# Splitting the weighted hidden block in the third and fourth layers' experts: VectorE writes the f16 first part of odd blocks itself

## The reference

```python
# L2: 14 experts, 128 -> 256 -> 128, one expert a token
logits = x @ router_w
assignments = argmax(logits); weights = softmax(logits)[assignments]
hid = gelu(einsum('nd,edf->nef', x, w1) + b1)
all_out = einsum('nef,efd->ned', hid, w2) + b2
moe_out = all_out[assignments] * weights
# L3: 8 experts, 128 -> 256 -> 128, two experts a token
h1 = gelu(einsum('bsd,edf->ebsf', mla_out, w1) + b1)
h2 = einsum('ebsf,efd->ebsd', h1, w2) + b2
moe_out = einsum('bse,ebsd->bsd', combine, h2)
# and for both: x = x + tanh(g_ffn[l]) * ...
```

## Time and profile before

| What | us |
|---|---|
| Median of 3 runs | 1422.92 |
| Lowest and highest of them | 1414.69, 1425.28 |
| The profiled execution, its own time | 1416.76 |
| Its span, first to last instruction | 1415.0 |
| First and last activation of the third layer's experts | 842.1, 1003.6 |
| First and last activation of the fourth layer's experts | 1313.7, 1402.6 |

### The profile page before, as it was taken

One profiled execution on the slowest core, in us unless ns is written; L12 is line 12 of the kernel. 1 busy time (PEld: TensorE's weight loads), 2 busy tenths in 40 slices (PEclk: granted clock), 3 DMA queues, 4 the chain that ended last, 5 costly groups with the idle time before them and its releaser, 6 DMA issues. The chain is left out here.

```text
span 1415.0 us, 30558 instructions
## 1 busy us (share of the span) xinstructions
PE 1113.4 (79%) x10422; PEld 531.6 (38%) x10422; DVE 909.6 (64%) x1691; ACT 786.6 (56%) x1467; POOL 551.7 (39%) x604
## 2 busy tenths in 40 slices
PE   2668767886299999998577759999868856777897
PEld 1334444444234444444222333333434532234333
DVE  3768648885656676666689534445668757983454
ACT  1257412773255555554178548888527723883886
POOL 1205102541145555554135127787401201211686
PEclk7779967998599999999689969999969985997999
DMA  8731004100044434442711023223142013100432
GB/s 250 252 131 34 2 1 151 41 26 1 7 134 132 127 123 132 125 129 67 245 32 32 2 40 90 92 93 91 64 163 63 3 47 108 45 17 2 103 92 75
DMA packets 108553, 119.05 MB, mean 84 GB/s; under 512 B 18114, under 2 KB 77690, under 8 KB 107154
## 3 DMA queue, kind: packets, MB, share of 16 engines
q1 hardware_dynamic: 106146, 104.16, 24.6%
q10 hardware_dynamic: 2288, 13.31, 2.6%
HBM read 98.30 MB, written 18.79 MB: 83 GB/s over the span
## 5 line engine op out<-in xcount | busy, mean ns | idle before, releaser
L1276 POOL TENSOR_TENSOR work<-Ks,work 128x512 f16<-128x512 f32 x308 | 356.2, 1157 | 231.4 <-ACT work L1353 222.9
L733 ACT ACTIVATE work<-ps 128x384 f32<-128x384 f32 (+1 forms) x640 | 304.0, 533 | 187.5 <-PE ps L589 116.8
L830 DVE TENSOR_REDUCE bmax<-ps 128x6 f32<-128x768 f32 (+1 forms) x320 | 334.6, 1056 | 84.1 <-PE ps L567 57.3
L1287 PE MATMUL ps<-ao,wf 128*128 128x512 f16 x1320 | 340.5, 384 | 12.9 <-DVEq L1374 6.6
L1397 DVE TENSOR_TENSOR Ks<-ps,Qs 128x512 f32<-128x512 f32 x304 | 210.1, 692 | 148.4 <-ACT ps L1345 131.1
L1303 PE MATMUL ps<-work,wf 128*128 128x512 f16 x924 | 250.9, 380 | 4.4 <-POOL work L1276 3.5
L1287 PEld LDWEIGHTS ps<-ao,wf 128*128 (+1 forms) x1320 | 120.7, 99 | 189.3 <-issue 54.6
L1353 ACT CAST work<-Ks 128x512 f16<-128x512 f32 x308 | 187.7, 610 | 3.9 <-DVE Ks L1397 3.5
L868 POOL TENSOR_SCALAR mx<-bmax 128x16 f16<-128x16 f32 x80 | 24.9, 311 | 381.1 <-DVE bmax L836 214.9
L578 PE MATMUL ps<-Qs,Ks 32*128 32x256 f16 x640 | 121.7, 290 | 60.3 <-DMA Qs<-mxT 25.6
L611 PE MATMUL ps<-work,V 128*9 128x256 f32 (+1 forms) x2560 | 154.7, 361 | 0.0
(11 more groups left out here) (162 smaller groups left out, 1376.2 us busy)
## 6 DMA issues: line engine op xcount, KB each, us to landing
Qs<-scrC SPq DMA_DIRECT2D x256, 128.0 KB, 3.0
Qs<-scrC SPq DMA_DIRECT2D x88, 256.0 KB, 3.1
Qs<-scrQ SPq DMA_DIRECT2D x40, 256.0 KB, 3.2
Ks<-scrK SPq DMA_DIRECT2D x40, 256.0 KB, 3.4
scrK<-work SPq DMA_DIRECT2D x60, 128.0 KB, 2.1
scrQ<-work SPq DMA_DIRECT2D x60, 128.0 KB, 2.3
Qs<-mxT SPq DMA_DIRECT2D x320, 1.0 KB
wf<-in_L_w ACTq DMA_DIRECT2D x2, 1792.0 KB, 12.0
```

Of the source, the lines that this page charges most:

```text
L733: act.activation(prob[:, g % 8, 0:W1], ps[:, 4 + g % 3, 0:W1], ACT.Exp, scale=float(att["dk"]) ** -0.5).then_inc(exped, 1)
L830: dve.tensor_reduce(bmax[:, n // 4 % 2, 2 * (n % 4):2 * (n % 4) + 2, 0:NB], ps[:, b0:b0 + 2, 0:W1].rearrange("p i (n w) -> p i n w", n=NB) ...
L1276: pool.tensor_tensor(hparts[:, (m + r) % 4, 1, :], weighted(m + r), hparts[:, (m + r) % 4, 0, :], ALU.subtract).then_inc(second, 1)
L1287: ins = pe.matmul(out, weight_parts(which, wpart, j), xh[:, xpart, c * CH:(c + 1) * CH], start=(i == 0), stop=(i == 2))
```

## The change

For l = 2 and 3, blocks with odd r get their f16 first part from VectorE: after the f32 product it makes the same product a second time, with f16 output into `hparts[.., 0]`, and only then counts `weighed`. As `hparts` is now written there, VectorE waits for `down` first (block b - 4's down matmuls). ScalarE copies the even blocks alone, at its odd steps, and counts `first` by 2. GpSimd waits for `first` on even blocks and for `weighed` on odd ones. The last copy after all chunks falls away, as the last block is odd. TensorE's list, the loads of SP and the gated layer are the same.

```diff
             def split(c, s, r):
                 m = N * c
-                pool.wait_ge(first, s + (m + 1))
+                if gated:
+                    pool.wait_ge(first, s + (m + 1))
+                elif r % 2 == 0:
+                    pool.wait_ge(first, s + (m + 2))
+                else:
+                    pool.wait_ge(weighed, s + (m + 3))
                 pool.tensor_tensor(hparts[:, (m + r) % 4, 1, :], weighted(m + r),
                                    hparts[:, (m + r) % 4, 0, :], ALU.subtract).then_inc(second, 1)
...
                 act.wait_ge(down, s + m)
                 act.wait_ge(weighed, s + (m + 2))
-                act.copy(hparts[:, (m + r - 1) % 4, 0, :], weighted(m + r - 1)).then_inc(first, 1)
+                act.copy(hparts[:, (m + r - 1) % 4, 0, :], weighted(m + r - 1)).then_inc(
+                    first, 1 if gated else 2)
...
                     activate(c, s, r)
-                    if c > 0 or r > 0:
+                    if (c > 0 or r > 0) and (gated or r % 2 == 1):
                         first_part(c, s, r)
...
-            first_part(NC, 0, 0)
+            if gated:
+                first_part(NC, 0, 0)
             copy_output(NC - 1)
...
-                dve.tensor_tensor(h1, h0, coef, ALU.mult).then_inc(weighed, 1)
+                if gated or r % 2 == 0:
+                    dve.tensor_tensor(h1, h0, coef, ALU.mult).then_inc(weighed, 1)
+                    return
+                dve.wait_ge(down, s + (m + 1))
+                dve.tensor_tensor(h1, h0, coef, ALU.mult)
+                dve.tensor_tensor(hparts[:, (m + r) % 4, 0, :], h0, coef, ALU.mult).then_inc(weighed, 1)
```

## The result

| What | us |
|---|---|
| Kernel before, median of 4 runs | 1421.83 (1414.69 to 1425.28) |
| Changed kernel, median of 4 runs | 1450.66 (1440.48 to 1454.46) |
| Ratio, with its 95% interval | 1.0198 (1.0133 to 1.0264) |
| Profiled execution of the changed kernel, own time and span | 1451.27, 1449.3 |
| The same kernel again, 6 runs, beside 11 of before (experiment 7) | 1443.46; 1.0118 (1.0071 to 1.0164) |

Slower, as forecast; 1441 was forecast, with 1423 to 1452 as the range. The forecast's sum was +21.4; the two comparisons give +28.8 and +18.8 as differences of medians.

The account below looks back on a forecast made before the run. A loop through ScalarE's copy and GpSimd's split, 1.36 us a block, was taken to bound the kernel, hardly above TensorE's 1.30. +4.7 + 17.3 - 0.6 = +21.4 on 1416.76 gives 1438.2; with part of an offset 1441, range 1423 to 1452.

Parts of the forecast that it names:

- The forecast's sum: Whole kernel: fourth layer +4.7, third layer +17.3, stage ends -0.6, together +21.4 us on the profiled 1416.76.
- The loop of copy and split: Before the change, ScalarE's copy and GpSimd's split hold up the down matmuls: at least 1.36 us a block.
- TensorE's own 1.30: Up and down matmuls of one block on TensorE take 1.30 us; nothing can go below it.
- The loop through the product: Up matmul, activation, VectorE products, up matmul two blocks later: 2.34 us grows by 0.60 to 2.94, exceeding TensorE's 2.60.
- Rival B: Faster: the second product fits VectorE's room and TensorE runs at 1.30 a block; 1399 us, chance 0.08.
- Copy loop after the change: Copy and split no longer bind: the even block's split ends 0.25 us before its down matmuls' turn.
- Fourth layer's chunk: Fourth layer's experts: 8 pairs of 2.94 plus 0.2 and 0.1, so 23.8 us against 22.63, +1.2 a chunk.
- Third layer's chunk: Third layer's experts: pairs of 3.27 in the register loop, chunk 45.2 us against 40.88; with product wait 0.69, pairs of 3.16.
- rival A: Third layer's register work hides: product at 0.69, up at 0.05, pairs 3.03; total +10, 1428 us, chance 0.15.
- At the end of each stage: The last block's copy goes, its split starts about 0.3 us earlier; two stages, -0.6.
- Rival C: VectorE's second product starts only after the first ends: 88 x 0.09 = 8 us more, 1449, chance 0.05.
- rival D: TensorE's pauses let the granted clock fall from 1.00 to 0.50, adding some 20 us: 1460, chance 0.03.

Follow-up runs that it names:

- experiment 7: Six runs each: changed kernel 1443.46; changed kernel with down distance four and four PSUM banks 1398.78; kernel before with both 1400.21; kernel before 1424.61 us.
- experiment 4: Kernel before, down matmuls four blocks behind the up matmuls instead of three in the third and fourth layers: 1400.78 against 1426.97 us, ratio 0.9885.
- experiment 6: Kernel before with down matmuls four blocks behind and four PSUM banks for the up matmuls: 1396.99 against 1426.97 us, ratio 0.9840.
- experiment 2: Changed kernel with four PSUM banks for the up matmuls instead of two, waits for the products two blocks lower: 1417.64 us, ratio to before 0.9929.
- experiment 5: Changed kernel with the second product over 128 of 512 columns: 1425.20 us, 1.0006; with one more whole product on odd blocks: 1497.99 us, 1.0547.
- experiment 3: Changed kernel with down matmuls four blocks behind the up matmuls instead of three: 1440.51 us, ratio to before 1.0122.
- experiment 1: The change in one layer alone, against the kernel before (1422.75 us): third layer only 1440.35, ratio 1.0113; fourth layer only 1424.36, ratio 1.0028.

## Why the prediction was right, point by point

**What bounded before.** Shown. The loop of copy and split was read as 1.36 a block from the rows; a distance of four took each 0.16 pause away (experiment 4), and TensorE's own 1.30 came out as the floor in four profiles of three kernels (experiments 4, 6 and 7): 21.8 us a chunk, the very number of the prediction.

**The loop through the product.** Shown from three sides. Its length in the fourth layer was put at 2.94 a pair and is 2.96; experiment 2 takes the release away from it and the loss disappears; experiment 5 moves its length down and up. The prediction named 0.26 as what the second product may add before it costs; at 0.20 it cost nothing and at 0.60 about 20 us, so the turn lies somewhere between. Rival B is out: VectorE had the room on average, not in this loop.

**Copy loop after the change.** The prediction had it 0.25 early, and experiment 3 finds no effect of it on the fourth layer. From 899 to 943 us and from 1367 to 1390 no down group waits for GpSimd; the 4.2 us in its line above lie elsewhere.

**Fourth layer's chunk.** 23.8 forecast, 24.0 measured (the 24.4 starts from the early activation), +1.4 instead of +1.2. The term that was too small is the one for the bias matmuls: between odd activations around them the gaps are 1.94 + 1.30 = 3.24, where 2.60 + 0.53 = 3.13 was forecast; the other pairs are 0.02 over. Together that is the missing 0.2. The change in one layer alone gives the same numbers (experiment 1).

**Third layer's chunk.** 45.2 forecast, 44.5 measured (and 44.9 from the early activation). Here I took the wrong end of a bound that was stated: activation to first product 0.80, on the ground that the new wait for `down` is a third one. This loop in the changed kernel:

```profile
908.26 0.82 PE L1292 MATMUL ps<-ao,wf 128*128 128x512 f16 x3 [0.38 <-DVE work L1409]
...
909.27 0.66 ACT L1350 ACTIVATE ps<-ps,cols 128x512 f32<-128x512 f32 x1 [1.19 <-PE ps L1292]
...
909.97 0.69 DVE L1408 TENSOR_TENSOR Ks<-ps,Qs 128x512 f32<-128x512 f32 x1 [1.04 <-ACT ps L1350]
...
910.58 0.68 DVE L1409 TENSOR_TENSOR work<-ps,Qs 128x512 f16<-128x512 f32 x1
...
911.42 0.82 PE L1292 MATMUL ps<-ao,wf 128*128 128x512 f16 x3 [0.40 <-DVE work L1409]
```

1.01, then 0.70, then 0.61 + 0.68, then 0.16: 3.16 a pair, the other end. So it wasn't the number of waits that made the 0.80 of the earlier trace rows: that row is of an even block, and in the kernel before the odd ones of the same loop, with two waits, mostly have 0.69 to 0.70. After the change the odd blocks have three waits and still 0.70, the even ones 0.80 or more. What differs is the value waited for: `down` is compared with the same value as the activation's count, the coefficient rows of the even blocks with one of their own. The sequencer's records on the two lines, L1395 for the coefficients and L1407 for `down`:

```profile
L1395 DVEq FUSED_REGOPS  x48: 46/57/64, 860.3 to 1028.9; - x48
L1407 DVEq EVENT_SEMAPHORE  x88: 21/50/50, 852.2 to 1435.8; - x88
```

The first has 48 register operations (shortest, median and longest in ns), the second has none. This fits, but no experiment takes the two apart. What made the chunk come out near all the same is a term that the prediction left out: in each of the loop's three turns one pair takes 3.31 or 3.32 instead of 3.16. In its odd block (5, 13 and 21 of a chunk) the first product comes 0.85 after the activation instead of 0.70; I saw it only in the changed kernel. The pair with the bias matmuls takes 3.32 as well. The 0.18 taken for the release of the up matmuls was near (0.16). So of rival A one half came true, the product at 0.69 to 0.70, and the other, the up matmuls at 0.05, did not: with pairs of 3.16 and not 3.03, A as a whole is out.

**At the end of each stage.** The -0.6 did not come. From the last activation to the last group of down matmuls it is 3.60 us before in both layers (1003.55 to 1007.15, 1402.64 to 1406.24) and 3.59 after (1030.09 to 1033.68, 1436.72 to 1440.31). The last split stands behind the one before it on GpSimd, which the sum had left out.

**The rule of the Trainium skill.** "VectorE: DVE Perf Modes", section "The DRAIN you can't avoid", has the next operation wait for an empty pipe, but the same paragraph goes on: "A next op that is not held starts earlier". The prediction took the first half alone. The runs agree with the second: of three products in a row each starts 0.60 to 0.61 after the one before, inside its recorded 0.68 to 0.69. Rival C, 8 us more, is out.

**The clock.** The granted clock is 1.00 in both stretches of the changed kernel shown above, though TensorE is recorded idle for 0.20 us a pair in the fourth layer and 0.38 to 0.40 in the third: rival D is out once a stage is under way. At its start it is another matter. In both kernels the third layer's experts begin at a clock of 0.50. In the kernel before it is 0.82 from 846 to 850 us and 1.00 behind that; in the first profile of the changed kernel it is 0.50 from 850 to 862 and 0.97 from 862 to 866. Its first chunk took 47.3 us, 6.2 more than before. In the second profile (experiment 7) that chunk took 44.4, but the fourth layer's first one 26.4 instead of 23.0, with 0.50 from 1340 to 1344. Whether the change delays this rise or the profiles differ by chance is open.

**The sum.** By the chunks the stages cost 4 x 4.0 + 4 x 1.6 = 22 us (21 with the two early activations set right), against +21.4 forecast; from first to last activation, with the first chunks in, 18.1 + 4.9 = 23.0 in the first profile and 23.3 in the second. That it comes so near is in part luck: 0.11 too much in each pair of the third layer's loop stands against the turns of the loop, the bias matmuls, the -0.6 and the slow first chunks, which were too little or left out. The +28.8 of the first comparison is more, +18.8 of the second less; in the first one's profile the other stages, whose code is the same, took 1176.0 us against 1164.6 before. Over the twelve profiles beside the one of before these other stages run from 1158.8 to 1178.6. That difference is chance in the main; that no microsecond of it belongs to the change is not shown.

## What to carry to other kernels

Before giving an idle engine a second piece of work, find what waits for the end of the first piece: count the signal's position in the loop that frees the buffer, not the engine's busy share. Write each loop's length down as a sum of rows and set it against the time in which it must close. The change is free up to the slack and costs its full price beyond; here the slack was 0.36 us a pair against the pace of before, 2.70, and 0.26 against TensorE's own 2.60. And where an engine is nearly full and yet pauses, look at the distance between producer and consumer first: one block more of it, and two unused PSUM banks, gave 24 us where moving work between engines lost about 20. When chunks are timed by one event, take one in the middle of a chunk: the first activation made two of the numbers above 0.4 us too long.

## What was unexpected of the hardware

The whole time spreads more than the work does: while chunks repeat within some 0.1 us between kernels, the stages that nobody touched differ by up to 20 us between profiles (1158.8 to 1178.6). The granted clock differs with it: its mean over the span is 0.871 in the profile whose other stages took 1178.6 and 0.892 in that with 1158.8. An effect of under 1% can't be read here from the whole time without many runs, and can from the stage.

A product over 128 columns is recorded with 0.28 us and one over 512 with 0.68 to 0.69, but behind a product of 512 either starts at the same 0.60 to 0.61: when the second may start doesn't depend on its own length. What starts directly behind the short one was not seen.
